# Six decoder layers as one unrolled pipeline instead of blocks and a loop, with one transpose job moved inside its unit

## What is computed

```python
def mha(xq, xkv, W, B, mask):
    q, k, v = proj(xq, W[0], B[0]), proj(xkv, W[1], B[1]), proj(xkv, W[2], B[2])
    score = jnp.einsum('bhqd,bhkd->bhqk', q, k) / math.sqrt(DH)      # 16 heads of 16
    if mask is not None:
        score = jnp.where(mask[:, None] == 0, -10000.0, score)
    out = jnp.einsum('bhqk,bhkd->bhqd', jax.nn.softmax(score, axis=-1), v)
    return merge_heads(out) @ W[3] + B[3]

for l in range(6):
    trg = layer_norm(trg + mha(trg, trg, sa_w[l], sa_b[l], mask))
    trg = layer_norm(trg + mha(trg, enc, ca_w[l], ca_b[l], None))
    trg = layer_norm(trg + relu(trg @ w1[l] + b1[l]) @ w2[l] + b2[l])
```

## Time and profile before

| | |
|---|---|
| median of three runs | 5195.07 us |
| the profiled execution | 5196.5 us |
| its span, first to last instruction | 5194.3 us |
| matmul busy, whole span | 4231.0 us (81%) |
| weight loads busy | 3145.5 us (61%) |
| VectorE busy | 2779.0 us (53%) |
| ScalarE busy | 1882.7 us (36%) |
| GpSimd busy | 308.7 us (6%) |
| mean granted TensorE clock | 0.896 |
| decoder: first and last cross-attention unit's maximum | 977.8 and 3193.1 us |

### The profile page before, as it was taken

How to read it: one execution, slowest core, us unless ns; L and a number is a source line. 1 busy time by engine, 2 the same in 40 slices (tenths; PEclk the granted TensorE clock), 3 DMA queues, 4 the chain that set the end, 5 groups by cost and what they waited for, 6 DMA issues and landing times. The chain is left out here.

```text
span 5194.3 us, 96901 instructions
## 1 busy us (share of the span) xinstructions
PE 4231.0 (81%) x39298; PEld 3145.5 (61%) x39298; DVE 2779.0 (53%) x5804; ACT 1882.7 (36%) x5127; POOL 308.7 (6%) x562
## 2 busy tenths in 40 slices
PE   6996695799999899999999997539588777877763
PEld 4664585577777677677677775338445576555533
DVE  2335411566666666666666674751267545244447
ACT  1222131344444344444444443102166444244421
POOL 0000101000000000000000000010111000000000
PEclk9998798899999999999999998859799788888876
DMA  2000165201101101101101100018544200000000
GB/s 99 26 26 18 51 221 191 68 26 44 50 18 44 51 26 36 51 26 36 51 30 40 50 18 16 1 51 294 183 153 148 90 0 22 17 17 24 9 1 8
DMA packets 112157, 302.45 MB, mean 58 GB/s; under 512 B 28856, under 2 KB 74616, under 8 KB 87168
## 3 DMA queue, kind: packets, MB, share of 16 engines
q1 hardware_dynamic: 108672, 288.28, 16.3%
q0 software_dynamic: 3072, 8.39, 0.5%
HBM read 281.68 MB, written 14.94 MB: 57 GB/s over the span
## 5 line engine op out<-in xcount | busy, mean ns | idle before, releaser
L2264 ACT ACTIVATE layers_probs<-banks,layers_negmax 128x257 f32<-128x257 f32 x768 | 358.2, 472 | 1156.4 <-DVE layers_negmax L2148 1156.4
L2000 PE MATMUL banks<-weights_a,ctx_tiles 128*128 128x256 f32 x1536 | 389.1, 386 | 92.2 <-ACT layers_sa_nT L2237 92.2
L1994 PE MATMUL banks<-ctx_tiles,weights_a 128*128 128x257 f32 x1536 | 406.6, 388 | 0.0
L2000 PEld LDWEIGHTS banks<-weights_a,ctx_tiles 128*128 128x128 f32 x1536 | 284.1, 192 | 143.2 <-ACT layers_sa_nT L2237 108.8
L2054 PE MATMUL banks<-layers_KT,layers_qblk 32*64 32x257 f32 x3072 | 267.1, 418 | 47.2 <-issue 25.5
L1994 PEld LDWEIGHTS banks<-ctx_tiles,weights_a 128*128 128x128 f32 x1536 | 274.3, 194 | 46.4 <-issue 18.9
L2128 DVE TENSOR_TENSOR layers_V<-banks,rows_a 128x256 f32<-128x256 f32 x384 | 160.3, 418 | 265.5 <-PE banks L2000 265.4
L2148 DVE TENSOR_REDUCE layers_negmax<-banks 128x2 f32<-128x514 f32 x384 | 262.3, 683 | 63.5 <-PE banks L2054 63.3
L2062 PEld LDWEIGHTS banks<-const,layers_probs 128*128 128x128 f32 x1536 | 169.5, 146 | 158.5 <-issue 158.4
L2062 PE MATMUL banks<-const,layers_probs 128*128 128x128 f32 x1536 | 265.1, 298 | 0.0
L2269 ACT COPY layers_pT<-banks 128x512 f32<-128x512 f32 x384 | 223.8, 583 | 3.3 <-PE banks L2062 3.3
(11 more groups left out here) (709 smaller groups left out, 8623.2 us busy)
## 6 DMA issues: line engine op xcount, KB each, us to landing
ctx_tiles<-in_ctx SPq DMA_DIRECT2D x66, 1028.0 KB, 4.9
weights_a<-in_L_w SPq DMA_DIRECT2D x44, 1024.0 KB, 5.3
l2x_B<-positions SPq DMA_DIRECT2D x32, 1280.0 KB, 5.9
weights_b<-in_L_w SPq DMA_DIRECT2D x32, 1024.0 KB, 6.4
weights_c<-in_L_w SPq DMA_DIRECT2D x16, 1024.0 KB, 7.2
weights_b<-in_L_xattn_w SPq DMA_DIRECT2D x12, 1024.0 KB, 7.4
ctx_tiles<-in_ctx_keys SPq DMA_DIRECT2D x32, 256.0 KB, 2.9
weights_c<-in_sa_w SPq DMA_DIRECT2D x24, 256.0 KB, 2.8
```

Source lines behind the costliest of these rows:

```text
L1994: last = mm(o[:, 0:LK], ca_wk[:, c, m * P:(m + 1) * P], E.ctx[:, tile % 2, c, j * LK:(j + 1) * LK], start=c == 0, stop=c == DC - 1)
L2000: last = mm(o[:, 0:D], E.ctx[:, tile % 2, c, first:first + P], ca_wv[:, c], start=c == 0, stop=c == DC - 1)
L2264: a(probs[:, cc, j, t], ps[:, t, 0:LK], ACT.Exp, bias=negmax[:, k % 2, t:t + 1], accum_out=totals[:, cc, t, j:j + 1]).then_inc(s["exp_done ...
```

## The change

The six blocks and the loop become one block over 51 steps. A place ("pos") is a tile of a layer, from 0 to 47; step i does self-attention of place i, the projections of place i-1, cross-attention of place i-2, and output and dense part of place i-3. That is the order of before, with all semaphore counts running through and waits on constants. The weights' sends keep their places in the steps. The values of the last key go into two buffers alternately, without a copy. In the first unit S0 is the last ring job instead of the first.

```diff
     UNIT_JOBS = [
-        [("S0", None, "act"), k_job(0), v_job(0), k_job(1), v_job(1)],
+        [k_job(0), v_job(0), k_job(1), v_job(1), ("S0", None, "act")],
         [("n", None, "act"), ("S1q", None, "dve"), k_job(2), ("S1k", None, "act"), k_job(3)],
...
-        def layer_block(layer, steps, carry, last):
...
-            loads = {} if last else loads_of(layer + 1)
...
-            with nc.Block(no_gpsimd_drain=True) as blk:
...
-                        if step == 0 and carry:
-                            sp.wait_ge(s["h_ca"], 1)
-                            send("w_ca_o")
-                            sp.wait_ge(s["h_dm"], 1)
-                            send("w_dm")
...
-                    for name in loads:
-                        sp.wait_ge(s[name], 16 * len(loads[name]))
...
-                        if it == first_ca * U + 2:
-                            if not carry:
-                                need_evacuated(dve, first_ca - 1, "X")
-                            v.tensor_copy(last_v[:, 0], last_v[:, 1]).then_inc(s["last_moved"], 1)
-                            dve.wait_ge(s["last_moved"], 1)
...
-            end_round(nc, handles)
...
-        steady = [parts(g, (g - 1) % NG, (g - 1) % NG, (g + 1) % NG, (g + 2) % NG) for g in range(NG)]
-        layer_block(0, [parts(sa=0), parts(sa=1, prep=0), dict(steady[0], out=None, dm=None)] + steady[1:], False, False)
-        with nc.Fori(1, NL - 1) as layer:
-            layer_block(layer, steady, True, False)
-        layer_block(NL - 1, steady[:6] + [dict(steady[6], sa=None), dict(steady[7], sa=None, prep=None), parts(out=7, dm=7)], True, True)
+        NPOS = NL * NG
+        steps = []
+        for step in range(NPOS + 3):
+            at_part = {"sa": step, "prep": step - 1, "ca": step - 2, "out": step - 3, "dm": step - 3}
+            steps.append({part: pos if 0 <= pos < NPOS else None for part, pos in at_part.items()})
+        N = len(steps)
...
+        later_loads = [loads_of(layer) for layer in range(1, NL)]
+
+        def need_weights(eng, name, pos):
+            layer = pos // NG
+            if layer and pos % NG == 0:
+                eng.wait_ge(s[name], 16 * len(later_loads[layer - 1][name]) * layer)
+
+        with nc.Block(no_gpsimd_drain=True) as blk:
...
+                for step in range(N):
+                    if 1 <= step <= NPOS:
+                        if step >= 2:
+                            need_job(sp, step - 2, "V", VC - 1)
+                        sp.dma_start(E.ctx[:, step % 2], A["ctx"][step % NG]).then_inc(s[f"ctx{step % 2}"], 16)
+                    layer, phase = (step + 1) // NG, step % NG
+                    if phase == NG - 1 and layer < NL:
+                        need_evacuated(sp, step, "S1q")
+                        need_evacuated(sp, step, "S1k")
+                        send(layer, "w_sa_qk")
+                        need_job(sp, step, "S2")
+                        send(layer, "w_sa_v")
+                        sp.wait_ge(s["h_sa"], step + 1)
+                        send(layer, "w_sa_o")
+                    if phase == 0 and 0 < layer < NL:
+                        need_evacuated(sp, step - 1, "q")
+                        send(layer, "w_ca_q")
+                        need_evacuated(sp, step - 1, "K", (DC - 1, GB - 1))
+                        send(layer, "w_ca_k")
+                        need_evacuated(sp, step - 1, "V", VC - 1)
+                        send(layer, "w_ca_v")
+                    if phase == 2 and 0 < layer < NL:
+                        sp.wait_ge(s["h_ca"], step - 2)
+                        send(layer, "w_ca_o")
+                        sp.wait_ge(s["h_dm"], step - 2)
+                        send(layer, "w_dm")
...
+                    if n >= RB:
+                        pe.wait_ge(s[evacuated[n - RB][0]], evacuated[n - RB][1])
+                    if kind in ("n", "S0", "D0"):
+                        need(pe, {"n": "h_sa", "S0": "h_dm", "D0": "h_ca"}[kind], pos - NG + 1 if kind == "S0" else pos + 1)
...
+                    if k % (NG * U) == GB - 1:
+                        need_evacuated(dve, pos, "X")
...
+                    elif kind == "X":
+                        need(act, "heads_ready", DC * (pos - NG))
+                        for m in range(DC):
+                            last = a(last_v[:, pos // NG % 2, m], o[:, m * NB:(m + 1) * NB], ACT.Identity, bias=ca_bv[:, m:m + 1])
...
+        end_round(nc, handles)
```

More of the change, by code:

```diff
@@ L1800, in decoder_layers @@
         s, handles = signals(st, nc, "layers", "job_done evac_dve evac_act scores_done max_ready exp_done transposed copied pv_done heads_ready "
-                             "spread_ready shares_done shifted last_moved soft_done pT_ready qblk_ready h_sa h_ca h_dm var_ready added_eps power_ready dve_step "
+                             "spread_ready shares_done shifted soft_done pT_ready qblk_ready h_sa h_ca h_dm var_ready added_eps power_ready dve_step "
                              "ctx0 ctx1 w_sa_qk w_sa_v w_sa_o w_ca_q w_ca_k w_ca_v w_ca_o w_dm")
@@ L2285, in parts @@
-        def parts(ca=None, out=None, dm=None, prep=None, sa=None):
-            return {"ca": ca, "out": out, "dm": dm, "prep": prep, "sa": sa}
-        steady = [parts(g, (g - 1) % NG, (g - 1) % NG, (g + 1) % NG, (g + 2) % NG) for g in range(NG)]
-        layer_block(0, [parts(sa=0), parts(sa=1, prep=0), dict(steady[0], out=None, dm=None)] + steady[1:], False, False)
-        with nc.Fori(1, NL - 1) as layer:
-            layer_block(layer, steady, True, False)
-        layer_block(NL - 1, steady[:6] + [dict(steady[6], sa=None), dict(steady[7], sa=None, prep=None), parts(out=7, dm=7)], True, True)
+        NPOS = NL * NG
@@ new lines, in decoder_layers @@
+        steps = []
[3 more added lines that the diff above has]
+        N = len(steps)
+        jobs, at = [], {}
+        for step, parts in enumerate(steps):
+            for u in range(U):
+                for kind, arg, engine in UNIT_JOBS[u]:
+                    pos = parts[PART[kind]]
+                    if pos is not None and (kind != "X" or pos % NG == 0):
+                        at[pos, kind, arg] = len(jobs)
+                        jobs.append((step, u, kind, arg, engine))
@@ new lines, in decoder_layers, with jobs_in, need, need_evacuated @@
+        evacuated = []
+        seen = {"dve": 0, "act": 0}
+        for job in jobs:
+            seen[job[4]] += 1
+            evacuated.append(("evac_" + job[4], seen[job[4]]))
+        by_unit = {}
+        for n, job in enumerate(jobs):
+            by_unit.setdefault(job[0] * U + job[1], []).append((n, *job))
+        def jobs_in(it):
+            return by_unit.get(it, [])
+        def need(eng, name, n):
+            if n > 0:
+                eng.wait_ge(s[name], n)
+        def need_evacuated(eng, pos, kind, arg=None):
+            name, n = evacuated[at[pos, kind, arg]]
+            eng.wait_ge(s[name], n)
@@ new lines, in need_job, with ca_unit @@
+        def need_job(eng, pos, kind, arg=None):
+            eng.wait_ge(s["job_done"], at[pos, kind, arg] + 1)
+        def ca_unit(it):
+            pos = it // U - 2
+            if not 0 <= pos < NPOS:
+                return None
+            return it - 2 * U, pos, it % U // GB, it % GB
+        later_loads = [loads_of(layer) for layer in range(1, NL)]
[3 more added lines that the diff above has]
+                eng.wait_ge(s[name], 16 * len(later_loads[layer - 1][name]) * layer)
```

653 lines of the change are left out of this document (285 added, 368 removed).

## The result

The changed kernel takes 5111.21 us (median of four runs, 5107.22 to 5113.55) against 5192.39 us of the kernel before in the same comparison: a ratio of 0.9847, with a 95% interval of 0.9831 to 0.9862. That is 81 us less. Forecast were 5107.5 us, 87.5 us less than the 5195.07 us known then; 6 us of that gain are missing. The profiled execution after has a span of 5108.6 us.

The account below looks back on a forecast made before the run. TensorE was taken to bound decoder steps but for one stall. Job order 28.5, removed boundaries 37 and fewer clock falls 22 sum to 87.5 us, from 5195.07 to 5107.5 us; range 5092 to 5134.

Parts of the forecast that it names:

- The bound: In a normal decoder step TensorE sets the time: 43.05 us of work plus one stall of 2.26 us.
- Rival 2: TensorE is not the bound in the rest of the step; 0.62 us returns at a later wait; 5136 to 5158 us; chance 0.08.
- Part 1: First unit of a step: S0's job goes last, saving 0.62 us in each of 46 steps, 28.5 us (25 to 35).
- The restart: Behind the stall, from TensorE's restart to the next matmul: 0.37 us with S0 (0.22 to 0.45), against 1.07 with V.
- S0's copy: ScalarE's copy of S0 moves behind both K evacuations, still over 1 us ahead of its first reader in the next unit.
- Part 2: No blocks and no loop: five boundaries' pauses and the half-rate clock behind them go, 37 us gained (30 to 38).
- The weight loads: At layer changes the last load lands 0.5 us before its V; costed at nothing, 5 us if late by 1 us.
- Part 3: Clock falls behind the stall: 7 of 21 stay, 14 x 1.55 = 22 us gained (33 gained to 4 lost).
- The sign named for this: In the profile after the change: fewer than ten steps with a mean clock of 0.96.
- rival 1: The falls of the clock stay despite the shorter stall: 28.5 + 37 - 4, 5134 us; chance 0.17.
- The slower side: Straight code must be fetched, each block of it making TensorE stand; at 1 us each 5300 us; chance 0.02.

## Why the prediction held, point by point

The time was 3.7 us from the forecast, closer than its terms were. A part of this is the starting point: before had 5195.07 us when the forecast was made and 5192.39 in the comparison, so the gain was 6.3 us from the forecast.

- **The bound.** That TensorE sets the step but for one stall was right. In the kernel with the norms moved, no other wait takes its place, and 42.78 of 42.84 us are matmuls. Rival 2, that the gain would be given back at a later wait, is out. By the rule of the Trainium skill (Perfetto Trace Analysis, Identifying the Most-Contended Engine) there is headroom left, since the weight loads are busy for 32.53 of 42.84 us, 76%; the runs show that no other engine sets the step, not that the matmuls couldn't be arranged better.
- **Part 1.** 0.62 us a step was forecast, 0.59 measured. The restart was put at 0.37 us and is 0.36; the stall at about 1.7 us, and it is 1.7. In 45 whole steps that is 26.6 us, of 28.5 forecast for 46. S0's copy is covered by 1.2 us as worked out.
- **Part 2.** 37 us were forecast for five pauses. 2189.17 us of before, less 45 normal steps (2041.7), X (4.1), 21 falls (32.6 at 1.55 each) and the first and last place (35.7 and 38.2) leaves 36.9. The weight loads did not become waits: the last one is issued at 1640.43 and lands 6.2 us later, and its V starts at 1647.11 with no stall, 0.5 us behind the landing as worked out. But the number belongs to this kernel only. With the new order the same five pauses cost 34.2 us (2139.75 - 2115.35, and 7 against 13 falls of 1.64 us), and without the stall 47.5. That a stall behind the pause takes up part of the half-rate stretch is my reading of it, argued and not isolated.
- **Part 3 is the term that was mis-sized.** I took a third of the falls to stay, 7, and 13 did. 21 x 1.55 less 13 x 1.64 is 11.2 us in place of 22; and there is one new fall in the decoder's first place, which got 1.1 us longer. The sign named for this, fewer than ten steps at a mean clock of 0.96, did not come. The only ground had been one row with a stall of 1.81 us, and it was no ground: at 1.7 us, falls come in more than a quarter of the steps. What the falls did lies between the forecast (7) and rival 1 (all stay and a few come), 6 above the one and 8 below the 21 of before. That they get fewer with a shorter stall was right: both kernels with a stall of 1.7 us have fewer than those with 2.26 us.
- **What made up for it.** 26.6 + 36.9 + 11.2 - 1.1 = 73.6 us in the decoder (73.8 measured), 14 less than forecast. The profiles' other stages gave 12 us back, no term of the forecast, at least in part by scatter. In medians of runs the gain is 81 us. The total was right by some luck.
- **The slower side.** No fetch of code shows: with the old order the straight pipeline has normal steps of 45.36 to 45.37 us as the loop had, and the fetched bytes fell.

Forecasting only what the change does, I saw in the rows that the maximum stood behind two norms, and took it as a fact. It was worth more than the change: the best kernel here, with pipeline and norms moved, takes 4998 us.

## What to carry to other kernels

When a bound engine stalls once per step, follow the release back until it meets work that nobody is waiting for; here two norms ahead of a maximum cost 2.5 us a step and their reordering gained more than a new pipeline and a new job order together (140 against 81 us). A job order that gives the stalled engine something to do is only a patch for that; it was worth nothing here once the stall was gone. Price a pause with what stands behind it: the same five cost 34, 37 and 47 us in three kernels.

## What the runs showed of the hardware

The granted clock falls to its lower level (0.50, which is 1.2 of 2.4 GHz) behind stalls of TensorE that are short and regular: in 25 of 44 steps with 2.26 us, in 13 of 44 with 1.7 us, in none with 0.4 us. A fall costs 1.5 to 1.65 us here, two thirds of the longer stall and nearly all of the shorter, and no stall is listed for it: it shows only as longer matmuls and as a mean clock of 0.96. The same stall in like steps is followed by a fall in one and not in the next, so its length alone doesn't settle it: with the same 1.7 us it was 13 and 13 of 44 steps in two profiles of the changed kernel and 7 of 39 with the pauses in between. That this hangs on how the steps lie in time is my reading, not isolated.

At a pause between blocks TensorE stands for 4.7 to 4.9 us where code follows in line and for 8.4 to 8.9 us where the loop turns (four profiles of kernels with blocks). In the kernel with the norms alone, the two steps around a pause are together 6.3 and 7.7 us longer in line, and 10.9 to 11.4 us longer where the loop turns, than two normal ones and X.
